# Graph network in five dense layers: forward counts dropped, count layers read the backward counts through a transposing DMA

## The reference, cut to what matters

```python
# block 1: edges in both directions, unit weights
src2 = concat([src, dst, loop]); dst2 = concat([dst, src, loop])
agg  = segment_sum(x[src2] * dis[src2] * dis[dst2], dst2)
x    = layernorm(x + relu(agg @ W.T + bias))
# block 2: one direction, unit weights
agg  = segment_sum((x @ W)[row] * dinv[row] * dinv[col], col)
x    = layernorm(x + prelu(agg + b))
# block 3: one direction, edge weights, three convolutions
h = relu(conv(x)); h = relu(conv(h)); x = layernorm(x + conv(h))
```

## Time and profile before

| | us |
|---|---|
| median of 3 runs | 4233.52 |
| lowest, highest | 4227.99, 4246.55 |
| span of the profiled execution | 4951.5 |
| build stage, narrow part | 62 to 418 |
| build stage, wide part | 418 to 1864 |
| left-over edges and GRU | 1864 to 2026 |
| l1 | 2026 to 2600 |
| l2 | 2600 to 3060 |
| l3a, l3b, l3c | 3060 to 4951.5 |

### The profile page before, as it was taken

How to read it: one execution, slowest core, us unless ns; L and a number is a source line. 1 busy time by engine, 2 the same in 40 slices (tenths; PEclk the granted TensorE clock), 3 DMA queues, 4 the chain that set the end, 5 groups by cost and what they waited for, 6 DMA issues and landing times. The chain is left out here.

```text
span 4951.5 us, 80811 instructions
## 1 busy us (share of the span) xinstructions
PE 3982.0 (80%) x30230; PEld 2665.0 (54%) x30230; DVE 2602.2 (53%) x5064; ACT 1548.4 (31%) x3170; POOL 2555.5 (52%) x2363
## 2 busy tenths in 40 slices
PE   5787787787788887388887886899888899887888
PEld 5677776677677775244443343444444455443444
DVE  7676555555555556555452334355435556513554
ACT  3334554445455564100000000223134334302332
POOL 4665544554555520266645664566256556505663
PEclk6777878888788888699998998899999999988999
DMA  4445555555566664699976664778655555527776
GB/s 147 125 130 163 190 188 182 189 188 189 186 193 200 196 211 147 188 321 322 303 255 188 204 206 140 272 277 291 223 179 186 175 179 176 190 93 259 261 276 244
DMA packets 612892, 1019.37 MB, mean 206 GB/s; under 512 B 90888, under 2 KB 417575, under 8 KB 612111
## 3 DMA queue, kind: packets, MB, share of 16 engines
q1 hardware_dynamic: 476700, 773.91, 45.6%
q0 software_dynamic: 90848, 199.74, 13.9%
q10 hardware_dynamic: 44956, 40.55, 2.6%
HBM read 737.12 MB, written 276.78 MB: 205 GB/s over the span
## 5 line engine op out<-in xcount | busy, mean ns | idle before, releaser
L951 POOL DMA_INDIRECT x<-p_table,src_i x832 | 953.8, 1146 | 826.0 <-DVE x L711 541.3
L1540 POOL DMA_INDIRECT rows_b<-x_table,low_src x552 | 585.0, 1060 | 540.5 <-POOLq L159 203.6
L930 ACT CAST st_cnt<-ps_mat 128x512 bf16<-128x512 f32 (+1 forms) x825 | 445.7, 585 | 520.8 <-PE ps_deg L845 239.7
L1619 PE MATMUL po_l3b<-mat_l3b,rows_b 128*128 128x512 f32 (+1 forms) x1372 | 580.7, 570 | 32.5 <-DMA mat_l3b<-weights_fwd 25.2
L1540 POOL DMA_INDIRECT rows_a<-h_table,low_src x412 | 441.7, 1072 | 302.1 <-DVE split_l3b L1831 178.2
L860 PE MATMUL ps_mat<-rows_a,hot_s 128*128 128x128 bf16 x4851 | 416.6, 244 | 135.1 <-issue 97.7
L860 PEld LDWEIGHTS ps_mat<-rows_a,hot_s 128*128 128x128 bf16 x4851 | 337.6, 111 | 180.1 <-issue 118.3
L1619 PE MATMUL po_l3a<-mat_l3a,rows_a 128*128 128x512 f32 (+1 forms) x882 | 390.5, 589 | 47.0 <-DMA mat_l3a<-weights_fwd 37.2
L1619 PE MATMUL po_l3c<-mat_l3c,rows_a 128*128 128x512 f32 (+1 forms) x882 | 390.5, 590 | 29.3 <-DMA mat_l3c<-weights_fwd 25.2
L1619 PEld LDWEIGHTS po_l3b<-mat_l3b,rows_b 128*128 128x128 f32 x1372 | 247.6, 200 | 258.5 <-issue 231.4
L1619 PE MATMUL po_l<-mat_l,rows_a 128*128 128x512 bf16 (+1 forms) x1323 | 298.2, 380 | 106.3 <-DVE mat_l L1859 87.1
(11 more groups left out here) (419 smaller groups left out, 7215.9 us busy)
## 6 DMA issues: line engine op xcount, KB each, us to landing
weights_fwd<-st_wt SPq DMA_DIRECT2D x396, 256.0 KB
mat_l<-counts_fwd SPq DMA_DIRECT2D x112, 896.0 KB
mat_l3a<-weights_fwd SPq DMA_DIRECT2D x56, 1792.0 KB
mat_l3c<-weights_fwd SPq DMA_DIRECT2D x56, 1792.0 KB
counts_rev<-st_cnt SPq DMA_DIRECT2D x588, 128.0 KB
rev_l<-counts_rev SPq DMA_DIRECT2D x84, 896.0 KB
mat_l3b<-weights_fwd SPq DMA_DIRECT2D x42, 1792.0 KB
counts_fwd<-st_cnt SPq DMA_DIRECT2D x396, 128.0 KB
```

The source lines that it names most:

```text
L930: nc.scalar.copy(st_cnt[:, q, :, j * 2 * P:j * 2 * P + n_col], ps_mat[:, f % 3, :].rearrange("p (d c) -> p d c", d=2)[:, :, 0:n_col]).then ...
L951: pool.indirect_dma_start(ring[:, j % RING, t * FD:(t + 1) * FD], None, p_table, bass.IndirectOffsetOnAxis(src_i[:, j * TH + t:j * TH + t ...
L1540: pool.indirect_dma_start(ring[:, j % RL, t, :], None, table, bass.IndirectOffsetOnAxis(low_src[:, j * TH + t:j * TH + t + 1].bitcast(U32), 0)
L1619: mm = nc.tensor.matmul(po[:, p % 2, k, 0:nb * P].rearrange("p (d c) -> p d c", c=P), rows[:, s, k * P:(k + 1) * P], cols, start=(s == 0 a ...
```

## The change

`counts_fwd` is gone, in HBM, in the fills and in the stores. The wide part has two fills for a sub-step: the backward counts of both pairs, then the weights; the degree matmuls with the source block as weights (L841 before) stand in the second fill in the wide part. There are four staging places instead of three. l1 and l2 get `counts_rev` as their forward matrix and read it with `dma_start_transpose` on SyncE's queue: the source is seen as (blocks x 128 rows) by 896 columns, and lands as 7 runs of up to 512 elements on 128 partitions. The layout of `mat` in these two layers is changed to suit it (slice first, then block), and so are VectorE's addition and TensorE's view of it. The second half of the one-hots covers 11 pairs instead of 12 places.

```diff
-STAGES = 3
+STAGES = 4
...
             def fill_of(u, s, part):
 
-                return fills_before(u) + (s if u < NARROW else 3 * s + min(part, len(sub_pairs(s))))
+                return fills_before(u) + (s if u < NARROW else 2 * s + part)
...
-                        n = 2 * HALF if h == 0 else NK + 1 - 2 * HALF
+                        n = 2 * HALF if h == 0 else NK - 2 * HALF
...
+                        f = fill_of(u, s, 0)
+                        if f >= 3:
+                            pe.wait_ge(evicted, f - 2)
                         for j, k in enumerate(sub_pairs(s)):
-                            f = fill_of(u, s, j)
-                            if f >= 3:
-                                pe.wait_ge(evicted, f - 2)
-                            b = f % 3
-
-                            rev_at = 2 * P * j if u < NARROW else 2 * P
                             rows = hot_d[:, h, j0 + j, :]
                             halves = [q for q in range(2) if 2 * k + q < NB]
-                            for q in halves:
-                                half = hot_s[:, h, j0 + j, q * P:(q + 1) * P]
-                                if u >= NARROW:
-                                    nc.tensor.matmul(ps_mat[:, b, q * P:(q + 1) * P], half, rows, start=True, stop=True)
-                                nc.tensor.matmul(ps_deg[:, 2 * k + q:2 * k + q + 1], half, slots[:, u % 2, NV, k, 0:1],
-                                                 start=False, stop=False)
+                            if u < NARROW:
+                                for q in halves:
+                                    nc.tensor.matmul(ps_deg[:, 2 * k + q:2 * k + q + 1],
+                                                     hot_s[:, h, j0 + j, q * P:(q + 1) * P], slots[:, u % 2, NV, k, 0:1],
+                                                     start=False, stop=False)
...
+                                    nc.tensor.matmul(ps_deg[:, 2 * k + q:2 * k + q + 1], half,
+                                                     slots[:, u % 2, NV, k, 0:1], start=False, stop=False)
                                     for v in range(3):
...
+                        f = fill_of(u, s, 0)
                         act.wait_ge(filled, f + 1)
-                        to = st_cnt[:, q, 1, 0:w] if u < NARROW else st_wt[:, q, 0:w]
-                        nc.scalar.copy(to, ps_mat[:, f % 3, 0:w]).then_inc(evicted, 1)
+                        nc.scalar.copy(st_cnt[:, q, 0:w], ps_mat[:, f % 3, 0:w]).then_inc(evicted, 1)
+                        if u >= NARROW:
+                            act.wait_ge(filled, f + 2)
+                            nc.scalar.copy(st_wt[:, q, 0:w], ps_mat[:, (f + 1) % 3, 0:w]).then_inc(evicted, 1)
...
-                            sp.dma_start(counts_fwd[u, :, cols], st_cnt[:, q, 0, 0:sub_cols(s)]).then_inc(staged_out[q], 16)
+                            sp.wait_ge(evicted, fill_of(u, s, 1) + 1)
                             sp.dma_start(weights_fwd[u, :, cols], st_wt[:, q, 0:sub_cols(s)]).then_inc(staged_out[q], 16)
...
+                                    else:
+                                        sp.dma_start_transpose(mat[:, q, :, 0:nb * P], own_cols.rearrange("d p m -> (d p) m")
+                                                               ).then_inc(mat_in[q], 16)
...
-            V.tensor_tensor(to, to, rev[:, n % REVS, :, 0:nb * P].rearrange("p s (d c) -> p d s c", c=P),
-                            ALU.add).then_inc(chunk_ready, 1)
+            V.tensor_tensor(to, to, rev[:, n % REVS, :, 0:nb * P], ALU.add).then_inc(chunk_ready, 1)
...
-        layer("l1", "relu", 1, FD, planes_of(rows_a), (counts_fwd, counts_rev), self1, dis1, l1b, dis2, [l1w[:]],
+        layer("l1", "relu", 1, FD, planes_of(rows_a), (counts_rev, counts_rev), self1, dis1, l1b, dis2, [l1w[:]],
...
-        layer("l2", "prelu", 1, FD, planes_of(rows_b), (counts_fwd,), self2, dis2, l2b, dis3, [l2w[:]],
+        layer("l2", "prelu", 1, FD, planes_of(rows_b), (counts_rev,), self2, dis2, l2b, dis3, [l2w[:]],
```

More of the change, by code:

```diff
@@ L542, in build @@
             hot = sb("hot", [P, 4, TH, W], F32, c)
-            st_cnt = sb("st_cnt", [P, STAGES, 2, 4 * P], BF16, c)
+            st_cnt = sb("st_cnt", [P, STAGES, 4 * P], BF16, c)
             st_wt = sb("st_wt", [P, STAGES, 4 * P], F32, c)
@@ L588, in stores @@
             def stores(n):
-                return 1 if n // SUBS < NARROW else 3
+                return 1 if n // SUBS < NARROW else 2
             def place(u, s):
@@ L827, in blocks @@
                             pe.wait_ge(slots_ready, 2 * u + 2)
+                        f = fill_of(u, s, 0)
+                        if f >= 3:
+                            pe.wait_ge(evicted, f - 2)
                         for j, k in enumerate(sub_pairs(s)):
-                            f = fill_of(u, s, j)
-                            if f >= 3:
-                                pe.wait_ge(evicted, f - 2)
-                            b = f % 3
-                            rev_at = 2 * P * j if u < NARROW else 2 * P
                             rows = hot_d[:, h, j0 + j, :]
                             halves = [q for q in range(2) if 2 * k + q < NB]
-                            for q in halves:
-                                half = hot_s[:, h, j0 + j, q * P:(q + 1) * P]
-                                if u >= NARROW:
-                                    nc.tensor.matmul(ps_mat[:, b, q * P:(q + 1) * P], half, rows, start=True, stop=True)
-                                nc.tensor.matmul(ps_deg[:, 2 * k + q:2 * k + q + 1], half, slots[:, u % 2, NV, k, 0:1],
-                                                 start=False, stop=False)
-                            nc.tensor.matmul(ps_mat[:, b, rev_at:rev_at + len(halves) * P], rows,
+                            if u < NARROW:
[3 more added lines that the diff above has]
+                                                     start=False, stop=False)
+                            nc.tensor.matmul(ps_mat[:, f % 3, 2 * P * j:2 * P * j + len(halves) * P], rows,
                                              hot_s[:, h, j0 + j, 0:len(halves) * P], start=True, stop=True)
@@ L846, in blocks @@
                                                   start=False, stop=False)
-                            if u >= NARROW:
-                                mm.then_inc(filled, 1)
+                        mm.then_inc(filled, 1)
                         if u < NARROW:
-                            mm.then_inc(filled, 1)
                             return
-                        f = fill_of(u, s, 2)
+                        f = fill_of(u, s, 1)
                         if f >= 3:
@@ L923, in _ @@
                             act.wait_ge(staged_out[q], 16 * sum(stores(i) for i in range(q, n, STAGES)))
-                        for j, k in enumerate(sub_pairs(s)):
-                            f = fill_of(u, s, j)
-                            if u < NARROW:
-                                break
-                            act.wait_ge(filled, f + 1)
-                            n_col = min(2 * P, NP - k * 2 * P)
-                            nc.scalar.copy(st_cnt[:, q, :, j * 2 * P:j * 2 * P + n_col], ps_mat[:, f % 3, :].rearrange(
-                                "p (d c) -> p d c", d=2)[:, :, 0:n_col]).then_inc(evicted, 1)
-                        f = fill_of(u, s, 2)
+                        f = fill_of(u, s, 0)
                         act.wait_ge(filled, f + 1)
-                        to = st_cnt[:, q, 1, 0:w] if u < NARROW else st_wt[:, q, 0:w]
-                        nc.scalar.copy(to, ps_mat[:, f % 3, 0:w]).then_inc(evicted, 1)
+                        nc.scalar.copy(st_cnt[:, q, 0:w], ps_mat[:, f % 3, 0:w]).then_inc(evicted, 1)
+                        if u >= NARROW:
+                            act.wait_ge(filled, f + 2)
+                            nc.scalar.copy(st_wt[:, q, 0:w], ps_mat[:, (f + 1) % 3, 0:w]).then_inc(evicted, 1)
                         if place(u, s) is not None:
@@ L1397, in layer @@
             with ExitStack() as c:
-                mat = sb(f"mat_{name}", [P, slots, GB, CHK, P], MDT, c)
+                mat = sb(f"mat_{name}", [P, slots, GB, CHK, P] if exact else [P, slots, CHK, GB * P], MDT, c)
                 REVS = 3
@@ L1612, in chunk @@
                                 s = ch * CHK + j
-                                if has_fwd[p]:
+                                if exact:
                                     cols = mat[:, m % slots, 0:nb, j, :]
+                                elif has_fwd[p]:
+                                    cols = mat[:, m % slots, j, 0:nb * P].rearrange("p (d c) -> p d c", c=P)
                                 else:
```

16 lines of the change are left out of this document (8 added, 8 removed).

## The result

The changed kernel takes 4346.48 us (median of 4 runs, 4338.9 to 4362.43) beside 4231.02 for the kernel before (4 runs, 4227.99 to 4246.55): ratio 1.0273, 95% interval 1.0243 to 1.0303. It is slower by 115 us, and outside the range.

The account below looks back on a forecast made before the run. TensorE's stream was taken to bound the build's wide part, the DMA engines l1. Terms -97 - 76 - 16 - 10 + 57 = -142 us, scaled by 0.855 to -121, gave 4110 us; range 4025 to 4260.

Parts of the forecast that it names:

- Transposing loads in l1: In l1, transposing loads cost 57 us more in all, with ends of 0 and 183.
- Transposing loads in l2: In l2, a load of 3.8 us, three of them ahead, stays covered by a 7.3 us chunk: no cost.
- Forward matmuls, ScalarE's waits, issue: Build's wide part: TensorE's stream loses 97 us of forward matmuls, 76 of waits for ScalarE and 16 of issue time.
- the 80 named as a sign of being wrong: Wide part: waits for ScalarE over 80 us would show the prediction wrong; TensorE's under 40 us would show it right.
- Scaling by 0.855: Whole kernel: the median run is 0.855 of the profiled span, so the sum of -142 us becomes -121.
- Narrow part: Build's narrow part: the fourth staging place takes 10 us off waits, with ends of 0 and 25.
- the slow load: l1: transposing loads use up the gains at 6.4 us each; at three times the plain load, 4385 us; chance 0.16.
- the forecast's full gain: Build: all gains together, before the cost of l1's loads, are 199 us unscaled.
- the second rival: Build: ScalarE stays late or VectorE becomes the bound, leaving only 97 + 16 of gain, 4186 us; chance 0.13.

Follow-up runs that it names:

- l2t2: Changed kernel with transposing loads in l2 alone, l1 loading plainly and untransposed, on the slower chips: 4854.33 us, 0.9766 of the kernel before.
- plain: Changed kernel with its new build, but plain untransposed loads in l1 and l2, on the slower chips: 4887.36 us, 0.9728 of the kernel before.
- plain2: Changed kernel with plain untransposed loads in l1 and l2, in another set on the slower chips: 4856.25 us, 0.9739 of the kernel before.
- after2: The changed kernel, unaltered, timed again in another set on the faster chips: 4359.18 us, 1.0331 of the kernel before.
- b2: The kernel before, unchanged, run again for its profile on the faster chips: 4238.56 us (one run).

## Why the prediction was wrong

Two terms failed, and the time left the range because both did. Scaled as the forecast was, +57 for the loads in l1 is 49 us, and measured are 144: 95 too few. The 189 for the wide part are 162, and measured are 57: 105 too many. With l1 alone mis-sized the time would have been 4112 + 95 = 4207, with l2's 37 on top 4244, with the build alone 4217: all inside 4025 to 4260.

*Transposing loads in l1, +57 (the first step that failed).* The range of the cost, 0 to 3.27 us a load, was well drawn: measured are 3.3 on the engines, its upper end, and l1 grew by 133 us on kind 2, 136 to 144 on kind 1. The choice inside it was wrong. I took the gathers' rate because a transposing load "still has to read whole rows"; it moves 256-byte pieces. The Trainium skill's 261 GB/s ("DMA: Bandwidth & Descriptors", section "Latency and other measured facts") would be 3.5 us a load; here it is 5.7 to 6.1, about 150 to 160 GB/s, and 4.9 in `l2t2`, so the runs do not agree with it. The Trainium skill's "as fast as regular DMAs" ("Advanced Engine Details and Errata", section "X-Bar Transpose (TRN2)") does not hold here either: the same bytes took 1.7 to 2.2 times the engine time of plain loads.

*Transposing loads in l2, nothing.* Wrong on kind 1, +37 us; nearly right on kind 2, +3 to +12. The prediction asked if one load fits into a chunk of 7.3 us, as if the queue were alone. The better question is whether all the engines' time fits into the stage: before on kind 1, 0.70 x 400 = 280 us, and 163 more make 443; the stage was 400 and became 437. On kind 2, 0.61 x 460 = 281, and the 117 more of `l2t2` make 398 of 460: still covered. For l1 on kind 1 it is 0.91 x 564 = 513 + 186 = 699, where 700 to 707 were measured. On kind 1 these sums are bookkeeping and no test: the 163 and 186 are read from the very stages that they account for, and packets take longer in a full stage (the gathers' too, 28.7% against 21.8% above). With the price of a stage that has room, 4.9 us, l1 would have come to some 630 us. Why a load takes 5.7 to 6.1 in a full one is not shown.

*Forward matmuls, ScalarE's waits, issue: -189 (the second step that failed).* The step was "a microsecond taken off that stream is a microsecond off the stage". On kind 1 it is not: TensorE waits 18 us for ScalarE, the 1613 matmuls are gone, and TensorE's busy time fell by 95 (my 97), yet the stage gained only 53 to 60, since GpSimd was full. The price was off too, as the waits that I read stand in a profile of kind 2: before on kind 1, TensorE waited 52 us for ScalarE at L840, and the two largest groups had no "issue" wait:

```profile
L860 PE MATMUL ps_mat<-rows_a,hot_s 128*128 128x128 bf16 x4846 | 350.8, 223 | 8.7
L840 PE MATMUL ps_mat<-rows_a,hot_s 128*128 128x128 bf16 x1613 | 250.1, 221 | 58.9 <-ACT st_cnt L930 51.8 <-DVE rows_a L691 2.6 <-DVE hot_s L688 1.8
```

TensorE, busy 90% of the stage instead of 94%, was granted 0.91 instead of 0.97 in the mean, so more of it at 1.2 GHz. On kind 2 `plain` gave -117 in the wide part (1442 to 1325) and `plain2` -71 (1400 to 1329), in a stage whose old form took 1400 to 1487 us in four profiles; the whole kernels gave -148 and -127. TensorE still waited 67 us for ScalarE at L852 and, in the same view, 36 at L838: 103, over even the 80 named as a sign of being wrong.

*Scaling by 0.855.* This hid the second step. A profile 17% longer than the runs was read as the same execution slowed evenly. In which stage the 715 us sat could not be read from that trace; but the gain should have had a lower end for the case that it was the build's waiting.

*Narrow part, -10.* The first copy of weights, which marks its end, starts at 369.8 us before, and at 367.4 and 369.9 in the two profiles after: 0 to -2, the lower end.

Sum on kind 1, `after2` against `b2` (two chips): -57 in the wide part, 0 in the narrow, +144 in l1, +37 in l2, about -9 in stages that were not touched: +115, measured +116 between the profiled executions.

*The rivals.* The first, the slow load, had the place and the sign, with 0.16. Its break-even of 6.4 us a load was not reached; the load took 5.7 to 6.1. With the forecast's full gain, 199 x 0.855 = 170 us, the measured cost of 144 + 37 would have come out at +11, no change. It came out slower because the second rival, the build that gives less, held too, though by GpSimd, which it had not named: it had ScalarE or VectorE as what binds, and my own reading had GpSimd waiting. I had priced each beside the middle value of the other, and no case had both ends: -113 + 183 = +70, scaled +60, a time of 4293 before l2 is counted, already above the range.

## What to carry to other kernels

The larger part of a transposing load's price here was the time of its small pieces on the DMA engines; add it to the engine time of the whole stage (share times length), and compare that with the stage, not one load with one chunk. Near a full stage take the upper end of the price. Before taking time off the leading engine, add up busy and issue time of the next one: here GpSimd at 952 of 1050 us. If the profile is much longer than the runs, the surplus may sit in one stage, and gains read there are the first to doubt; and price two bad cases together once.

## What the runs showed of the hardware

- Two kinds of chips: the same kernel takes 4221 to 4231 us on one and 4968 to 5035 on the other. The old build's wide part takes 1050 against 1400 to 1487; l1 differs by 3%. Halving the gathers brings the new build's near each other (844 and 885 us).
- A transposing DMA of 512 rows by 896 columns of bfloat16 moves in 256-byte packets, and holds its queue 3.9 to 6.5 us at the median, where a plain one leaves after 0.37.
- Such a load takes 5.7 to 6.1 us of the 16 engines' packet time in l1 and l2 of the changed kernel on kind 1, and 4.9 in l2 on kind 2, where the plain load takes 2.8.
- The cost in l1 was nearly the same on both kinds, 133 and 136 to 144 us.
